# One decoder layer on one core: the router's statistics tile by tile and its rows six slots later, routing in five groups instead of four, the count five slots behind the ranks

## The chip, the core and the metric

The kernel runs on one core of a Trainium2 chip. Five engines run side by side, each its own queue in order, and wait for each other by semaphores: TensorE (PE, matmuls and transposes into eight PSUM banks), VectorE (DVE), ScalarE (ACT), GpSimd (POOL), and SyncE (SP), which issues DMAs. The metric is the device time of one execution in microseconds; less is better. Before the change it is 1469.41 us, the median of three runs (1467.95 to 1471.85).

## The reference

Eight sequences of 256 tokens with 512 features pass three residual blocks. Cut to what matters:

```python
x = x + ssm(layernorm(x))                          # state-space mixer, 64 heads
x = x + xattn(layernorm(x), ctx_512, ctx_512)      # 32 query heads, 8 key heads of 16
x = x + moe(layernorm(x))                          # 8 experts, two per token
# moe: router_input = x * rsqrt(mean(x*x) + 1e-6) * rsqrt(512) * router_scale
#      logits  = router_input @ router_logits       (512 x 8)
#      choices = top 2 of the logits;  weights = softmax probabilities / their sum over the two
#      tokens sorted by expert;  out = (gelu(x Wg) * (x Wu)) Wd * scale, added back by weight
```

All of it is float32 in the kernel's matmuls but for the attention scores, whose queries and keys are split in float16 parts.

## The kernel before, in words

The 2048 tokens are 16 tiles of 128 rows, two tiles per sequence b. All of x stays on the chip. Three stages follow each other: the mixer (to about 700 us), attention and routing (700 to 1014 us), the experts (39 tiles of gathered tokens, to the end).

The order of work is written out by hand. `attention_slots` builds a table from slot numbers to pieces of work, `put(s, piece, ...)` adds pieces to slot s, and every engine walks the same list and does its own part of each piece. So a piece's slot decides where it stands in the queue of each engine that has a part in it; what it waits for is in its code. Inside a slot the pieces stand in the order in which `put` was called. Slots 0 to 255 are the 256 score items, 32 for each sequence (`n = 32`). I call slots 32k to 32k+31 round k. In round k

- TensorE does one `score` (L1033) for sequence k and one `max` (L1018, two matmuls, for sequence k+1) per slot, and one `product` (L1042, eight matmuls in two groups of four heads' quads) for four slots;
- ScalarE does one `exponent` (L1114) per slot, VectorE one `max_fold` (L1216) per slot, both one slot behind;
- the row maxima of sequence k+1 end at slot 27 of the round: `nmax` and `n_turn` at slot 28, `n_copy` and its DMA `n_out` (L1458) at 29. The first score of round k+1 waits for that DMA;
- queries and keys of sequence k+2 are prepared: `q`, `q_hi`, `q_lo`, `q_turn`, `k_turn` and their copies in slots 2 to 24; in rounds 0, 2 and 4 VectorE also takes the layer norm statistics (`q_bn`) of four tiles.

The router's work on sequence b follows in round b+1, counted from f = 32(b+1): GpSimd adds the attention's result to x (`attend`, f+8); VectorE takes the statistics of both tiles (`r_stats`, f+12: two `bn_stats` L1252, two `bn_aggr` L1255, three small ones); GpSimd does three Newton steps for the reciprocal root (`r_newton`, f+12, 14 small instructions); ScalarE writes the normed rows of tile t (`r_xn`, L1133, f+16+2t), SyncE stores them (`r_store`); TensorE turns them (`r_turn`, L540, f+17+2t), ScalarE copies (`r_copy`, L1145), TensorE multiplies by the router's weights (`r_logit`, L1059, eight matmuls shown, f+19+2t), VectorE keeps the eight logits (`r_keep`, L1275). SyncE also writes x of both tiles to the output (`out_in`, f+20). For sequence 6 the rows start seven slots later (`late = 7`).

Routing is done in groups of tiles, `ROUTED = [(last sequence, first tile, end), ...]`. A group is a chain of small VectorE instructions: `c_scale` (and `c_newton` on GpSimd), `c_rank` (eight instructions, L1307 to L1314, whose size grows with the tiles), `c_count` (two matmuls on TensorE that wait for `c_rank`, L1068), `c_logit`, `c_exp` (ScalarE), `c_slots` (L1334 to L1341, one step per tile and five more), `c_weight` (five, L1322 to L1326). `place` (GpSimd, L1363) makes one 128x128 matrix per tile and choice. The last group and the last sequence's router come after slot 265, in a tail that ends with the first gather of tokens for the experts.

Five PSUM banks (`work_ps`) are dealt out in this order by `shared_banks`: a piece that opens a bank takes the one whose last reader stands earliest in the list, and TensorE waits for that reader. So TensorE can run at most a few `max` ahead of VectorE's `max_fold`.

## Time and profile before

| | |
|---|---|
| median of three runs | 1469.41 us (1467.95 to 1471.85) |
| profiled execution, its own time | 1465.78 us |
| its span from first to last instruction | 1464.0 us |
| mean granted TensorE clock | 0.954 of full |
| busy in the span: PE, DVE, ACT, POOL | 92%, 60%, 49%, 40% |
| rounds 0 to 7, start to start, us | 34.3, 34.3, 37.9, 34.1, 44.5, 35.8, 35.2, 27.9 |

How to read it: the span is what the profile measures, 1.8 us less than the execution's own time. The shares of the whole span say little about one stage: in the experts' stage PE is busy nearly all the time, while in the rounds of attention PE and DVE take turns at being the last to be ready. The rounds' lengths are the distances of their first exponents.

### The profile page before, as it was taken

To read this page: it belongs to the slowest core of one execution; us is meant where nothing else is said; L and a number is where in the kernel's file an instruction comes from. 1 tells how busy PE (TensorE), PEld (TensorE's weight loads), DVE (VectorE), ACT (ScalarE), POOL (GpSimd) and SP (SyncE) were. 2 spreads that over 40 slices of the span, in tenths; PEclk is the share of its full clock that TensorE was granted. 3 is DMA by queue.
4 is the path that set the end of the run, shared out by engine and by line. 5 is a ranking of instruction groups with operands and counts; after the bars stand their busy time and mean duration, and the time that the engine had idled before them with its cause. 6 is when DMAs were issued, how large, how long until landed. Compare 5 with 4: busy or idle time off the path is not lost.

```text
span 1464.0 us, 23008 instructions
## 1 busy us (share of the span) xinstructions
PE 1339.8 (92%) x7713; PEld 734.7 (50%) x7713; DVE 877.2 (60%) x1822; ACT 723.4 (49%) x1390; POOL 584.7 (40%) x871
## 2 busy tenths in 40 slices
PE   5799999999999999998788877888999999999997
PEld 4566666666666665654333333323444444444443
DVE  5798898979797979757888888755111111111111
ACT  2666667667666776663676766672111111111110
POOL 1454465555455465774223246143122222222221
PEclk9899999999999999998798988887999999999999
DMA  9000000000000000000210100002343344244322
GB/s 337 9 8 5 7 6 1 12 1 12 1 9 4 8 6 8 17 1 1 97 34 33 35 33 31 30 31 74 115 132 107 79 133 135 51 130 130 58 44 30
DMA packets 40291, 73.00 MB, mean 50 GB/s; under 512 B 18544, under 2 KB 22896, under 8 KB 39152
## 3 DMA queue, kind: packets, MB, share of 16 engines
q1 hardware_dynamic: 30240, 48.10, 9.4%
q0 software_dynamic: 8736, 20.61, 7.3%
q10 hardware_dynamic: 1200, 2.82, 0.5%
q8 instruction: 65, 1.06, 0.3%
q14 instruction: 50, 0.41, 0.1%
HBM read 148.91 MB, written 19.99 MB: 115 GB/s over the span
## 4 chain that ended last, share of the span: by engine, by line
PE 67%; DVE 18%; issue 5%; POOL 3%; ACT 3%; DMA 2%; SPq 1%; POOLq 0%; DVEq 0%; ACTq 0%
PE work_ps L535 13%; PE gate_ps L1524 9%; PE up_ps L1524 9%; PE down_ps L1508 9%; PE work_ps L607 7%; DVE conv L816 6%; PE work_ps L540 3%; PE work_ps L629 3%; DVE maxes L1216 3%; PE work_ps L1042 2%; PE mturn_ps L540 2%; PE decay_ps L1033 2%; PE decay_ps L617 2%; DVE mix L732 2%; DMA qT<-nmaxT 1%
## 5 line engine op out<-in xcount | busy, mean ns | idle before, releaser
L535 PE MATMUL work_ps<-xnT,w_in 128*128 128x256 f32 (+1 forms) x1216 | 301.0, 393 | 2.3 <-DVE xdt L856 1.5
L732 POOL TENSOR_TENSOR mix<-decay,cbm 128x512 f32<-128x512 f32 x128 | 182.1, 1424 | 218.9 <-ACT decay L727 191.0
L535 PEld LDWEIGHTS work_ps<-xnT,w_in 128*128 128x128 f32 (+1 forms) x1216 | 220.2, 189 | 64.9 <-issue 33.7
L723 ACT ACTIVATE decay<-decay_ps 128x512 f32<-128x512 f32 x256 | 154.1, 602 | 111.1 <-PE decay_ps L617 110.5
L1612 POOL DMA_INDIRECT out_dram<-y_out,ids x39 | 61.9, 1587 | 334.3 <-DVE row_w L1576 230.2
L1216 DVE TENSOR_REDUCE maxes<-work_ps 128x2 f32<-128x512 f32 x256 | 166.7, 683 | 42.8 <-PE work_ps L1018 41.8
L816 DVE SCALAR_TENSOR_TENSOR conv<-raw,conv_w,conv 128x256 f32<-128x256 f32 x240 | 179.2, 753 | 7.1 <-ACT conv L683 1.3
L1114 ACT ACTIVATE prob<-decay_ps 128x512 f32<-128x512 f32 x256 | 142.9, 608 | 78.9 <-PE decay_ps L1033 77.5
L1591 DVE TENSOR_TENSOR act<-gelu,up_ps 128x512 f32<-128x512 f32 x39 | 26.8, 688 | 252.1 <-PE up_ps L1524 252.1
L727 ACT ACTIVATE decay<-decay 128x512 f32<-128x512 f32 x256 | 164.0, 641 | 4.7 <-PE work_ps L535 3.0
L1524 PE MATMUL gate_ps<-w_e,xgT 128*128 x312 | 140.5, 593 | 1.4 <-ACT xgT L1541 1.0
L1508 PE MATMUL down_ps<-w_e,actT 128*128 x312 | 140.4, 593 | 0.8 <-ACT actT L1554 0.8
L1524 PE MATMUL up_ps<-w_e,xgT 128*128 x312 | 140.3, 592 | 0.0
L607 PE MATMUL work_ps<-w_out,yz 128*128 128x512 f32 x256 | 131.3, 637 | 4.5 <-DVE yz L874 3.7
L732 DVE TENSOR_TENSOR mix<-decay,cbm 128x512 f32<-128x512 f32 x128 | 102.5, 801 | 34.8 <-PE work_ps L629 19.2
L1033 PE MATMUL decay_ps<-qT,kT 49*128 49x512 f16 x256 | 94.0, 430 | 13.2 <-DMA qT<-nmaxT 8.2
L1583 DVE TENSOR_SCALAR y_out<-down_ps,row_w 128x512 f32<-128x512 f32 x39 | 29.3, 751 | 122.3 <-PE down_ps L1508 122.3
L1018 PE MATMUL work_ps<-kT,qT 48*128 48x256 f16 x512 | 94.2, 302 | 5.1 <-DVE maxes L1216 1.3
L1524 PEld LDWEIGHTS up_ps<-w_e,xgT 128*128 128x128 f32 x312 | 59.3, 190 | 74.6 <-issue 74.6
L629 PE MATMUL work_ps<-mix,xdt 128*32 128x128 f32 x2048 | 83.7, 282 | 8.4 <-DVE mix L732 7.6
L1541 ACT ACTIVATE xgT<-mturn_ps 128x512 f32<-128x512 f32 x39 | 23.3, 597 | 136.6 <-PE mturn_ps L540 136.6
L1042 PE MATMUL work_ps<-prob,v_aug 128*32 128x512 f32 x512 | 81.8, 716 | 9.6 <-DVE maxes L1216 8.9
(270 smaller groups left out, 1913.5 us busy)
## 6 DMA issues: line engine op xcount, KB each, us to landing
w_e<-c_experts_dram SPq DMA_DIRECT2D x39, 3072.0 KB
normed_tokens<-r_xn SPq DMA_DIRECT2D x17, 256.0 KB, 2.2
out_dram<-x_sb SPq DMA_DIRECT2D x17, 256.0 KB, 2.5
x_sb<-x_dram SPq DMA_DIRECT2D x1, 3072.0 KB, 16.6
w_in<-c_w_inT_dram ACTq DMA_DIRECT2D x1, 2560.0 KB, 12.3
w_in<-c_w_inT_dram SPq DMA_DIRECT2D x1, 2048.0 KB, 8.8
w_out<-c_w_outT_dram SPq DMA_DIRECT2D x1, 2048.0 KB, 21.6
RT<-cum_scratch SPq DMA_DIRECT2D x32, 48.0 KB
```

Of the source, the lines that this page charges most:

```text
L535: m = e.matmul(ps[0:width, at:at + L], w_in[:, k, col:col + width], xnT[b % 2][:, k, :], start=(k == 0), stop=(k == KD - 1))
L607: m = e.matmul(work(stage, tile)[:, :], yz[tile % 2][:, ct, :], w_out[:, ct, :], start=(ct == 0), stop=(ct == NCZ - 1))
L629: m = e.matmul(work("y", b, c, hf)[32 * quad:32 * quad + 32, ct * P:(ct + 1) * P], xdt[hf][:, 2 * HG * ct + h, :], mix[(s - 1 + h // HG) % ...
L723: e.activation(decay[s % 5][:, :], decay_ps[s % 3][:, :], ACT.Relu, scale=-1.0).then_inc(piece_done[stage], 1)
L727: e.activation(decay[s % 5][:, :], decay[s % 5][:, :], ACT.Exp, scale=-1.0).then_inc(piece_done[stage], 1)
L732: return e.tensor_tensor(four(mix[s % 5]), four(decay[s % 5]), cb, ALU.mult)
L816: m = e.scalar_tensor_tensor(o, raw[n % 2][:, i, k:k + L], conv_w[:, c, k:k + 1], o, ALU.mult, ALU.add)
L1033: e.matmul(score_ps[s % 3][:, :], kT[b % 3][base:base + PARTS + 1, k, t * P:(t + 1) * P], qT[b % 3][base:base + PARTS + 1, 2 * k:2 * k + 2 ...
L1114: e.activation(prob[s % 12][:, :], score_ps[s % 3][:, :], ACT.Exp, scale=DH ** -0.5).then_inc(piece_done[stage], 1)
L1216: e.reduce_max(maxes[b % 2][:, t, first:first + 2], work("max", b, p)[:, :].rearrange("p (h t) -> p h t", h=2), AX.X).then_inc(piece_done[ ...
L1508: m = e.matmul(down_ps[i % 2][:, :], actT[i % 2][:, k, :], w_e[:, bass.ds(place[i], 1), k, 2 * EH:].rearrange("p o n -> p (o n)"), start=( ...
L1524: m = e.matmul(ps[:, :], xgT[i % 2][:, k, :], w_e[:, bass.ds(place[i], 1), k, off:off + EH].rearrange("p o n -> p (o n)"), start=(k == 0), ...
```

## The change

Only the table of slots changes, and how the statistics are cut.

- `r_stats` is cut: the two `bn_stats` become pieces `r_bn` of their own at f+13 and f+15, one tile each, and `r_stats` (the `bn_aggr` and what follows) and `r_newton` move from f+12 to f+16.
- The router's rows and all that follows them (`r_xn`, `r_store`, `r_turn`, `r_copy`, `r_logit`, `r_keep`, `out_in`) move six slots later for sequences 0 to 5. Sequence 6 keeps its seven.
- `ROUTED` gets five groups. The first one of eight tiles at slot 148 (round 4, slot 20) is cut in two of four tiles, at slots 96 and 160 (rounds 3 and 5, slot 0). The group of tiles 8 to 11 stays at slot 224 (round 7, slot 0), that of 12 and 13 at slot 251, the last one in the tail.
- In the first three groups `c_count` and what follows stand five slots later than before relative to `c_rank`, and `c_weight` is 16 slots behind the group's start instead of 9. `place` follows each group at 17 slots from its start, eight in ten slots, instead of two every four slots.

```diff
-ROUTED = [(3, 0, 8), (5, 8, 12), (6, 12, 14), (7, 14, 16)]
+ROUTED = [(1, 0, 4), (3, 4, 8), (5, 8, 12), (6, 12, 14), (7, 14, 16)]
...
-        late = 7 if b == NB - 2 else 0
-        put(f + 12, ("r_stats", b), ("r_newton", b))
+        late = 7 if b == NB - 2 else 6
+        for t in range(TPB):
+            put(f + 13 + 2 * t, ("r_bn", b, t))
+        put(f + 16, ("r_stats", b), ("r_newton", b))
         for t in range(TPB):
             put(f + 16 + late + 2 * t, ("r_xn", b, t), ("r_store", b, t))
...
-    for g, at in enumerate((4 * n + 20, 7 * n, 7 * n + 27)):
+    for g, (last, first, end) in enumerate(ROUTED[:-1]):
+        at = n * (last + 2) if last < NB - 2 else 7 * n + 27
+        apart = 5 if last < NB - 2 else 0
         put(at, ("c_scale", g), ("c_newton", g))
-        put(at + 3, ("c_rank", g), ("c_count", g))
-        put(at + 5, ("c_logit", g), ("c_exp", g))
-        put(at + 6, ("c_slots", g))
-        if g < 2:
-            put(at + 9, ("c_weight", g), ("c_weight_out", g))
-    for t in range(12):
-        for c in range(2):
-            put(n * 5 + 4 * t if t < 8 else n * 7 + 8 + 4 * (t - 8) + 2 * c, ("place", c, t))
+        put(at + 3, ("c_rank", g))
+        put(at + 3 + apart, ("c_count", g))
+        put(at + 5 + apart, ("c_logit", g), ("c_exp", g))
+        put(at + 6 + apart, ("c_slots", g))
+        if apart:
+            put(at + 11 + apart, ("c_weight", g), ("c_weight_out", g))
+            for t in range(first, end):
+                for c in range(2):
+                    put(at + 12 + apart + 3 * (t - first) + c, ("place", c, t))
...
+            elif stage == "r_bn":
+                b, t = key
+                e.wait_ge(*done("attend", b))
+                own.settle(e.bn_stats(r_bn[:, t, :], x_sb[:, b * TPB + t, :]))
             elif stage == "r_stats":
                 b, = key
-                e.wait_ge(*done("attend", b))
-                for t in range(TPB):
-                    m = e.bn_stats(r_bn[:, t, :], x_sb[:, b * TPB + t, :])
-                own.settle(m)
                 for t in range(TPB):
                     m = e.bn_aggr(r_mv[:, b * TPB + t, :], r_bn[:, t, :])
```

The changed file is five lines longer above the engines' code, so a line L1114 of the kernel before is L1119 after.

Where it moves instructions, first on VectorE in round 1 (sequence 0): the statistics `r_bn`, `r_mv`, `r_rows` among the folds of the maxima (`maxes`) and the copies of keys, queries and outputs. Before:

```order
L1216 TENSOR_REDUCE maxes<-work_ps 128x2
L1252 BN_STATS r_bn<-x_sb 128x6 x2
L1255 BN_AGGR r_mv<-r_bn 128x2 x2
L530 TENSOR_SCALAR r_rows<-r_mv 128x2
L513 TENSOR_SCALAR r_rows<-r_rows 128x2
L514 TENSOR_SCALAR r_rows<-r_rows 128x2
L1216 TENSOR_REDUCE maxes<-work_ps 128x2
```

After:

```order
L1256 BN_STATS r_bn<-x_sb 128x6
L1211 COPY kT<-work_ps 128x8x128
L1221 TENSOR_REDUCE maxes<-work_ps 128x2 x2
L1256 BN_STATS r_bn<-x_sb 128x6
L1239 RECIPROCAL recip<-work_ps 128x16
L1247 TENSOR_TENSOR o_tok<-work_ps,recip 128x2x2x16 x4
L1221 TENSOR_REDUCE maxes<-work_ps 128x2
L1260 BN_AGGR r_mv<-r_bn 128x2 x2
L535 TENSOR_SCALAR r_rows<-r_mv 128x2
L518 TENSOR_SCALAR r_rows<-r_rows 128x2
L519 TENSOR_SCALAR r_rows<-r_rows 128x2
```

One block of seven instructions between two folds has become three blocks, with three folds, a key copy and an output piece between them.

Then on TensorE, round 1 again: the turn of the router's rows (`work_ps<-ident,r_xn`) and the router's matmul (`w_router`). Before, with queries (`ident,xnT`) and keys of the next sequences around them:

```order
L540 MATMUL work_ps<-ident,r_xn 128x128 x4
L540 MATMUL work_ps<-ident,xnT 128x128 x8
L1033 MATMUL decay_ps<-qT,kT 128x512
L1018 MATMUL work_ps<-kT,qT 128x256 x2
L1042 MATMUL work_ps<-prob,v_aug 32x512 x4
L1033 MATMUL decay_ps<-qT,kT 128x512
L1018 MATMUL work_ps<-kT,qT 128x256 x2
L1059 MATMUL work_ps<-w_router,r_xnT 128x8 x4
L540 MATMUL work_ps<-ident,r_xn 128x128 x4
L1033 MATMUL decay_ps<-qT,kT 128x512
```

After, with the turn of the maxima (`nmax`) behind them:

```order
L1064 MATMUL work_ps<-w_router,r_xnT 128x8 x4
L545 MATMUL work_ps<-ident,r_xn 128x128 x4
L1038 MATMUL decay_ps<-qT,kT 128x512
L1023 MATMUL work_ps<-kT,qT 128x256 x2
L1047 MATMUL work_ps<-prob,v_aug 32x512 x4
L1038 MATMUL decay_ps<-qT,kT 128x512
L1023 MATMUL work_ps<-kT,qT 128x256 x2
L1064 MATMUL work_ps<-w_router,r_xnT 128x8 x4
L1038 MATMUL decay_ps<-qT,kT 128x512
L1023 MATMUL work_ps<-kT,qT 128x256 x2
L1029 MATMUL work_ps<-ident,nmax 32x128 x2
```

The router's two turns and two products have left the stretch in which queries are turned, and stand in the round's last eight slots, right ahead of the turn of the maxima.

Last, ScalarE in round 1, the rows `r_xn` and their copies `r_xnT` among the exponents (`prob`). Before:

```order
L1133 ACTIVATE r_xn<-x_sb,r_rows 128x512
L1114 ACTIVATE prob<-decay_ps 128x512 x2
L1145 ACTIVATE r_xnT<-work_ps 128x512
L1133 ACTIVATE r_xn<-x_sb,r_rows 128x512
L1114 ACTIVATE prob<-decay_ps 128x512
L1108 ACTIVATE qT<-work_ps 128x8x128
```

After:

```order
L1107 ACTIVATE xbc<-xn 128x32x16
L1119 ACTIVATE prob<-decay_ps 128x512 x4
L1113 ACTIVATE qT<-work_ps 128x8x128
L1119 ACTIVATE prob<-decay_ps 128x512
L1126 ACTIVATE pv<-work_ps 128x512
L1119 ACTIVATE prob<-decay_ps 128x512 x2
L1138 ACTIVATE r_xn<-x_sb,r_rows 128x512
```

Six more exponents, a query copy and an output copy now stand ahead of the first row.

## Rows read from the trace of the kernel before

**Rows 1.** Windows: length, PE, PEld, DVE, ACT, POOL busy, clock, DMA; rounds, or stretches.

```profile
742.84:763.75 20.91, 18.45 (x167) 9.69 (x171) 17.63 (x42) 15.95 (x30) 8.46 (x20) 0.92 0.17 57
763.75:771.04 7.29, 4.78 (x43) 1.76 (x37) 6.06 (x15) 4.73 (x10) 0.00 (x0) 1.00 0.02 5
771.04:808.89 37.85, 31.93 (x253) 14.24 (x251) 30.84 (x77) 26.51 (x50) 13.13 (x38) 0.86 0.10 33
778.54:802.27 23.73, 20.72 (x170) 10.27 (x171) 18.06 (x45) 16.05 (x29) 10.22 (x28) 0.84 0.15 51
808.89:842.96 34.07, 27.29 (x253) 12.98 (x251) 28.92 (x68) 26.40 (x50) 10.42 (x24) 1.00 0.11 37
842.96:887.48 44.52, 33.88 (x255) 14.54 (x251) 39.22 (x112) 26.98 (x52) 17.23 (x52) 0.82 0.09 28
893.82:917.55 23.73, 19.67 (x167) 10.61 (x171) 18.50 (x42) 16.28 (x30) 18.34 (x34) 0.86 0.12 46
929.10:952.03 22.93, 19.04 (x112) 9.13 (x112) 13.96 (x36) 12.04 (x24) 5.06 (x16) 0.73 0.12 46
```

**Rows 2.** Chain that ended last, in round 1: start us, us, what.

```profile
746.27 1.21 DVE r_bn L1252 x2
...
752.02 0.23 POOL r_rows L1371
752.28 0.82 ACT r_xn L1133
...
767.23 3.34 DMA qT<-nmaxT
```

**Rows 3.** Waits, 702 to 990 us: who waited for whom, us in total, times, longest.

```profile
PE decay_ps L1033 <- DMA qT<-nmaxT: 8.2, 6, 1.9
...
PE work_ps L1024 <- DVE nmax L1222: 6.4, 6, 3.0
ACT r_xn L1133 <- POOL r_rows L1371: 5.9, 6, 2.7
...
PE work_ps L540 <- ACT r_xn L1133: 5.7, 6, 2.7
...
PE work_ps L1068 <- DVE chosen L1312: 3.7, 2, 3.5
...
ACT weight L1150 <- DVE weight L1298: 2.1, 2, 1.0
```

**Rows 4.** PE in order of time, round 1: router's matmuls and a turn, full clock.

```profile
755.89 1.06 PE L1059 MATMUL work_ps<-w_router,r_xnT 128*128 128x8 f32 x8
756.80 0.64 PE L540 MATMUL work_ps<-ident,r_xn 128*128 128x128 f32 x4
```

**Rows 5.** PE in order of time, round 6: the same two at half clock.

```profile
942.00 1.87 PE L1059 MATMUL work_ps<-w_router,r_xnT 128*128 128x8 f32 x8
943.73 1.09 PE L540 MATMUL work_ps<-ident,r_xn 128*128 128x128 f32 x4
```

**Rows 6.** DVE in order of time, round 7: a four-tile group, first and last of its steps.

```profile
957.21 0.15 DVE L1281 TENSOR_TENSOR mean_sq<-r_rows 128x4 f32<-128x4 f32 x1
...
958.08 0.42 DVE L1307 TENSOR_TENSOR larger<-logit 128x256 f32<-128x256 f32 x1
...
960.41 0.17 DVE L1314 TENSOR_SCALAR chosen<-rank 128x32 bf16<-128x32 f32 x1
...
962.14 0.17 DVE L1295 TENSOR_SCALAR mean_sq<-mean_sq 128x4 f32<-128x4 f32 x1 [1.56 <-POOL mean_sq L520]
...
964.63 0.17 DVE L1341 SCALAR_TENSOR_TENSOR place_of<-rounded,slot_of 128x8 f32<-128x8 f32 x1
...
965.53 0.18 DVE L1322 TENSOR_TENSOR weight<-weight,chosen 128x32 f32<-128x32 f32 x1
...
966.18 0.83 DVE L1325 TENSOR_TENSOR weight<-weight,mean_sq 128x32 f32<-128x32 f32 x1
967.04 1.19 DVE L1326 TENSOR_TENSOR weight<-weight,e_scale 128x32 f32<-128x32 f32 x1
```

More of the change, by code:

```diff
@@ L170, in mixer_slots @@
     return slots
-DMA_ONLY = {"freed", "mixed", "cum_out", "cum_in", "ctx_in", "n_out", "router_in", "first_expert", "r_store", "out_in", "c_weight_out", "keep_warm"}
+DMA_ONLY = {"freed", "mixed", "cum_out", "cum_in", "ctx_in", "n_out", "router_in", "first_expert", "r_store", "out_in", "c_weight_out", "keep_warm", "r_bn"}
 def bank_use(stage, *key):
@@ L284, in attention_slots @@
         put(f, ("last_stats", t), ("last_center", t))
-    put(f, ("last_newton",), ("c_weight", 2), ("c_weight_out", 2), *[("place", c, t) for t in (12, 13) for c in range(2)])
+    put(f, ("last_newton",), ("c_weight", 3), ("c_weight_out", 3), *[("place", c, t) for t in (12, 13) for c in range(2)])
     for stage in ("r_turn", "r_copy", "r_logit"):
@@ L289, in attention_slots @@
         put(f, ("r_xn", NB - 1, t), ("r_store", NB - 1, t), ("out_in", NB - 1, t), ("r_keep", NB - 1, t))
-    put(f, ("c_rank", 3), ("keep_warm", 1, 5), ("c_count", 3), ("keep_warm", 2, 11), ("c_logit", 3), ("c_exp", 3), ("c_slots", 3), *[("place", c, t) for t in (14, 15) for c in range(2)])
-    put(f, ("c_base",), ("c_spread", 0), ("c_weight", 3), ("c_weight_out", 3), ("c_spread", 1))
+    put(f, ("c_rank", 4), ("keep_warm", 1, 5), ("c_count", 4), ("keep_warm", 2, 11), ("c_logit", 4), ("c_exp", 4), ("c_slots", 4), *[("place", c, t) for t in (14, 15) for c in range(2)])
+    put(f, ("c_base",), ("c_spread", 0), ("c_weight", 4), ("c_weight_out", 4), ("c_spread", 1))
     return slots
```

## The prediction

> **What bounds the kernel now.** I read four things in this order: the windows of the rounds, the waits, the chain of one round, and single instructions in order of time. All that the change moves lies in rounds 1 to 7, so the mixer, the tail behind slot 265 and the experts keep their time, unless their first gather comes at another moment.
>
> In the middle of round 1 (20.91 us) TensorE is busy 18.45 and VectorE 17.63 [rows 1]: neither is the bound alone. They hand the time to each other. Up to the half of it VectorE is behind, since the folds, key copies, output copies and the statistics stand close; then TensorE is, with turns of queries, router rows and router products. The chain says so in round 1: `r_bn` of both tiles on VectorE 1.21, GpSimd's Newton steps to 752.25, the row `r_xn` 0.82 at 752.28, TensorE after it [rows 2]. The waits for this hand-over are ScalarE's for `r_rows`, 5.9 us in six waits, longest 2.7, and TensorE's for `r_xn`, 5.7 in six, longest 2.7 [rows 3]: one delay, told twice.
>
> In the closing (763.75 to 771.04, 7.29 us) TensorE is busy only 4.78 and VectorE 6.06 [rows 1]. There the folds of the maxima, the copy `nmax`, its turn, and the DMA `n_out` (3.34 us in round 1 [rows 2]) stand behind each other; the first score of the next round waits 8.2 us in six for that DMA, 1.4 each, and the turn of the maxima 6.4 in six for `nmax` [rows 3].
>
> Round 4 is the outlier: 44.52 us against 37.85 for round 2, which has the same other work; VectorE is busy 39.22 against 30.84 [rows 1]. That is the group of eight tiles: 8.4 us of VectorE work cost 6.67 us, 3.5 of it as one wait of TensorE's `c_count` for `chosen` [rows 3].
>
> The clock counts too: mean 0.84 in the middle of round 2, 0.82 in round 4, 0.86 in round 5's middle, 0.73 in round 6's [rows 1]. The router's product took 1.06 us at the full clock (2.4 GHz) and 1.87 at the half (1.2 GHz), a turn 0.64 and 1.09 [rows 4, 5].
>
> **The statistics and the rows, middle.** `r_bn` is the same work in two pieces, one more start: below 0.1 us, I take 0. With the rows six slots later, `r_xn` (slot 22) has some six exponents more between itself and the Newton steps, so the 5.7 us of waits go. The router's two turns and two products (2 x (0.5 + 1.0) = 3.0 us of TensorE at the full clock, taking a turn at 0.5 rather than the 0.64 that overlaps its neighbour) leave the middle, which then holds 15.4 us of TensorE work and is bound by VectorE: its 17.63 plus 1.0 of idle that I leave it. Bounds of that idle: 0, and the 3.3 that it has today. I take 1.0 because VectorE is short of work only where TensorE is behind, and TensorE has 3 us less.
> - Round 1: 17.63 + 1.0 = 18.6, against 20.91: -2.3. Round 3 has the same pieces and nearly the same length: -2.3.
> - Round 2: 18.06 + 1.0, plus 0.7 for statistics of x that wait for GpSimd, = 19.8, against 23.73: -3.9. Round 4 alike, its group apart: -3.9.
> - Round 5: 18.50 + 1.0 = 19.5 against 23.73: -4.2.
> - Round 6: 22.93, less the four pieces at the half clock (2 x (1.87 + 1.09) = 5.9), less 0.5 for the rest of its wait for `r_xn`: 16.5, -6.4. VectorE's 13.96 [rows 1] is no bound.
>
> Sum: -23.0 us.
>
> **The same pieces, closing.** Six closings (rounds 1 to 6) take 3.0 us of TensorE work more. Of round 1's idle (7.29 - 4.78 = 2.5) the wait for `n_out` can't be filled, since the router's products stand ahead of it; the wait for `nmax` (6.4 in six, the longest 3.0, in the others near 0.7) can. So +3.0 - 0.7 = +2.3 each, +13.9 in all. Bounds: +0.5, if all 2.5 of idle filled up, and +5.8, if the clock falls (below). The rows' stores (slots 22 to 26) now stand three to five slots ahead of `n_out` on the same queue, and two rows of 0.82 us on ScalarE stand among the exponents there: 0 to 1 us each, I take 0.3, +1.8 for six.
>
> **The groups.** Round 4 loses its group: -6.7. Rounds 3 and 5 get one of four tiles each. Its price is from round 7's, which has four tiles today [rows 6]: `c_scale` 957.21 to 958.17, 0.96; `c_rank` 958.08 to 960.58, 2.5; `c_logit` and `c_slots` 962.14 to 964.80, 2.7; `c_weight`, five instructions of 0.2 where nothing disturbs them, 1.0: 7.2 us of VectorE in all. What idle is there for it? In round 3 VectorE is busy 28.92 of 34.07; of the 5.15 idle I count 3.3 in the middle and 1.2 in the closing by round 1's rows, so 0.65 is left in the opening, where the group stands. To that comes about 0.8 at the round's start, in which VectorE waits for the DMA, and 0.5 of the middle's idle for `c_weight`: 7.2 - 0.65 - 0.8 - 0.5 = 5.2. Twice: +10.4. Round 4's own rate (6.67 for 8.4) would give 5.7 each. Together +3.7: two small groups in the stretches where VectorE is the bound cost more than a large one where it had some room. This step speaks against the change, and is half of why I forecast little.
>
> In round 7 `c_count` now stands five slots behind `c_rank` and `c_logit` behind the Newton steps, for which VectorE waited 1.56 us [rows 6]. ScalarE's wait for `weight` (2.1 in two [rows 3], 1.05 here) and 0.2 of TensorE's for `chosen` go: -1.2.
>
> In `c_weight` L1325 and L1326 took 0.83 and 1.19 us, where L1322, of the same shape, took 0.18; GpSimd was at work on the output's addition and on `place` there [rows 6]. The Trainium skill (SBUF — State Buffer, section "Who interferes with whom") says that a VectorE instruction with two SBUF inputs contends with a GpSimd instruction that reads SBUF; the trace agrees. If `c_weight` in rounds 3 and 5 met such work it would be 2.7 us instead of 1.0, and the sum 3.4 us higher. In the new order `place` stands a slot behind `c_weight` and can't start ahead of its place in the queue, and the addition (slot 8) is over; I leave it out.
>
> **The sum.** -23.0 + 13.9 + 1.8 + 3.7 - 1.2 = -4.8 us. The profiled execution took 1465.78 itself (its span 1464.0), so it would take 1461.0. The median of the runs shown is 1469.41, 3.6 above it; the difference carries over: 1464.6 us.
>
> **The rivals.** One in which nothing of this applies, that the rows aren't freed: `r_newton` ends where today's ended plus four slots, the rows start six later, so two slots are gained, about 2.3 us in a middle, against waits of 0.95 in the mean and 2.7 at most. Enough; only round 6 could keep 0.4 us. No rival with a chance of its own.
>
> *The clock falls in the closings (slower).* TensorE would be at 0.5 in the closings where VectorE has starved it ahead: rounds 3 and 5 (groups) and round 6, which is at 0.89 and below already. Then a closing's 7.8 us of TensorE work takes 1.87/1.06 = 1.76 times as long, +5.9; 1.8 to 2 of it lies under waits for `nmax` and `n_out` that shrink, so +3.9 each, +11.7 for three: 1476. For it: the half clock stands behind stretches in which TensorE waited, as in the middle of round 6 after 2.7 for `r_xn`. Against: the closing of round 1 had the clock 1.00 with only 4.78 of 7.29 busy [rows 1], and will be fuller. It decides from two closings on. The Trainium skill (TensorE: Matmul & The Clock Gate, section "What's actually happening") holds that the throttled clock is the default and activity releases it; round 1's closing, at 1.00 while a third idle, is no example of that rule either way, and the rule would make the fuller closing safe. Chance 0.20.
>
> *What leaves the middle comes back (same).* VectorE keeps 1.8 us of idle in each middle rather than 1.0, since the folds' banks tie it to TensorE slot by slot: +0.8 x 6 = +4.8, 1469.4. For it: today's idle is 3.3 with both engines near 18. Against: TensorE has 3 us less there. Chance 0.21.
>
> *The half clock goes (larger gain).* In rounds 4 and 6 it follows long waits, 3.5 for `chosen` and 2.7 for `r_xn`, which the change removes. If those stretches run at 2.4 GHz throughout, the rest of the two rounds' matmuls gains about 3 us each: 1458.5. Against: round 2 falls to 0.84 with no such wait. Chance 0.14.
>
> **How the numbers follow.** The forecast has 0.45, with its own range 1460 to 1468. A difference under 0.3% (4.4 us) can't be told from none here; the forecast lies just past that, so I give 0.29 of it to faster, 0.16 to the same. Faster: 0.29 + 0.14 + 0.01 of the second rival = 0.44. Same: 0.16 + 0.20 + 0.01 of the first = 0.37. Slower: 0.19. The range of 8 in 10: 1455, beyond the larger gain with its own error, to 1475, which leaves out half of the slower case.
>
> **What would show it.** In the profile after: no wait of `r_xn` for `r_rows`; no wait near 3.5 of `c_count`; rounds 1 to 7 of 34.6, 36.6, 39.6, 36.5, 39.4, 31.4 and 26.7 us; in the closings TensorE busy 7.8 at a granted clock near 1.00, and 9 to 10 us long. Closings of 12 or a clock of 0.5 there mean the first rival; middles of 19.5 us in rounds 1 and 3 the second; clocks of 1.00 in rounds 4 and 6 the third. The forecast is wrong in its largest term if the closings grow by less than 1 us, since 13.9 rests on TensorE having no room there; and in the groups if rounds 3 and 5 don't grow by 4 us and more.

## The result, and the profile after

| | before | changed |
|---|---|---|
| median, runs of the first comparison | 1470.63 us (4 runs, 1467.95 to 1476.6) | 1486.19 us (4 runs, 1484.51 to 1490.97) |
| ratio, 95% interval | | 1.0124 (1.0095 to 1.0154) |
| repeated on another occasion | 1466.26 us (29 runs) | 1476.14 us (12 runs, 1466.75 to 1490.89), ratio 1.0065 (1.0029 to 1.0101) |
| span of the profiled execution | 1464.0 us | 1484.5 us |
| its mean granted TensorE clock | 0.954 | 0.936 |

I forecast 1464.6 us, faster; it is slower by 0.65 to 1.2%. Of the 20.5 us between the two spans, 5.7 had arisen before round 0 began (round 0 starts at 702.41 and at 708.15 us), where no instruction was changed. Rounds 0 to 7 account for 14.6 more (284.0 against 298.6 us), the tail and the experts for 0.2. So about a quarter of the distance between these two profiles arose where the change moves nothing: ahead of round 0 the same instructions ran at a mean granted clock of 0.96 instead of 0.97. The medians in the table are of all runs; the ratios leave out the runs over 1.5% above the fastest of their kernel (two of the changed kernel's twelve).

First windows of the kernel before that were not shown: rounds 1, 5, 6 and 7, and the closings of rounds 2 and 5 (columns as in [rows 1]: length, then PE, PEld, DVE, ACT, POOL busy, the granted clock).

```profile
736.75:771.04 34.29, 28.28 (x253) 13.32 (x251) 29.11 (x68) 26.39 (x50) 10.45 (x24) 0.95 0.11 36
887.48:923.30 35.82, 29.89 (x253) 14.33 (x252) 29.47 (x68) 26.83 (x51) 21.27 (x38) 0.89 0.09 31
923.30:958.50 35.20, 29.38 (x191) 12.54 (x188) 23.90 (x66) 21.49 (x40) 6.03 (x19) 0.81 0.08 31
958.50:986.41 27.91, 23.73 (x138) 8.70 (x138) 15.88 (x74) 20.90 (x42) 16.47 (x48) 0.90 0.11 40
...
802.27:808.89 6.62, 4.79 (x43) 1.76 (x37) 5.47 (x14) 4.74 (x10) 0.00 (x0) 1.00 0.02 5
...
917.55:923.30 5.75, 4.79 (x43) 1.70 (x37) 5.31 (x14) 4.73 (x10) 0.00 (x0) 1.00 0.02 6
```

The same view of the changed kernel, rounds 1 to 7:

```profile
740.78:778.40 37.62, 33.45 (x253) 14.23 (x251) 29.14 (x68) 26.97 (x51) 10.46 (x24) 0.82 0.09 33
778.40:820.88 42.48, 38.46 (x253) 16.08 (x249) 30.84 (x77) 26.93 (x50) 13.18 (x38) 0.72 0.08 29
820.88:863.53 42.65, 34.63 (x252) 14.46 (x254) 35.73 (x100) 27.37 (x53) 19.64 (x44) 0.84 0.09 30
863.53:901.57 38.04, 32.57 (x253) 14.30 (x251) 31.68 (x83) 27.04 (x50) 13.19 (x38) 0.87 0.09 33
901.57:947.08 45.51, 39.07 (x255) 16.64 (x251) 35.61 (x94) 27.50 (x51) 19.46 (x44) 0.74 0.07 25
947.08:976.20 29.12, 24.96 (x190) 10.18 (x188) 24.43 (x67) 21.49 (x42) 6.59 (x21) 0.96 0.10 38
976.20:1006.76 30.56, 26.54 (x138) 8.90 (x138) 15.62 (x73) 21.00 (x42) 15.86 (x46) 0.78 0.11 36
```

Compare rounds 1 and 2 with the rows before. VectorE has nearly the same work (29.11 and 29.14, 30.84 and 30.84), and TensorE shows the same 253 matmuls, but is busy 33.45 instead of 28.28 and 38.46 instead of 31.93: the work is the same and the mean clock is lower, 0.95 to 0.82 and 0.86 to 0.72. How much of a round's length is the clock and how much the new order, these rows alone don't tell. With two levels, 0.5 and 1, a mean of 0.72 over 42.48 us is 23.8 us at the half clock. Summed over rounds 1 to 7 that makes about 57 us before and 101 after.

Where I had put the gain and the loss, the changed kernel's middles of rounds 1, 2 and 6, and the closings of rounds 1, 2, 5 and 6 behind them:

```profile
748.71:768.65 19.94, 17.57 (x151) 8.08 (x148) 17.63 (x41) 15.45 (x28) 7.39 (x19) 0.91 0.04 14
768.65:778.40 9.75, 8.35 (x58) 3.44 (x60) 5.81 (x15) 5.62 (x12) 0.00 (x0) 0.82 0.23 84
786.26:809.39 23.13, 20.36 (x151) 9.10 (x148) 18.02 (x41) 15.79 (x29) 9.99 (x27) 0.78 0.03 12
809.39:820.88 11.49, 11.32 (x58) 4.75 (x58) 5.14 (x14) 5.42 (x11) 0.00 (x0) 0.55 0.20 71
935.61:947.08 11.47, 11.30 (x58) 4.77 (x58) 5.14 (x14) 5.43 (x11) 0.00 (x0) 0.55 0.20 71
953.01:967.96 14.95, 12.07 (x96) 4.86 (x97) 14.38 (x36) 11.21 (x22) 5.08 (x16) 1.00 0.05 20
967.96:976.20 8.24, 7.99 (x50) 3.36 (x49) 4.49 (x19) 5.55 (x12) 0.81 (x3) 0.87 0.26 97
```

Before, the middle of round 1 was 20.91 and its closing 7.29 [rows 1]. The closings of rounds 2 and 5 are TensorE busy for all but 0.17 us of 11.5, at 0.55 of the clock. Round 6's middle, where half clock went (0.73 before, 1.00 now), is 8.0 us shorter.

The changed kernel has a second profile (after_again below, its own time 1486.49 us). In it the closings of all of rounds 1 to 5 are like those two. Here are rounds 1, 3 and 5; rounds 2 and 4 took 11.1 us at 0.56:

```profile
761.72:773.25 11.53, 11.29 (x58) 4.73 (x58) 5.14 (x14) 5.43 (x11) 0.00 (x0) 0.56 0.23 82
847.03:858.54 11.51, 11.29 (x58) 4.74 (x58) 5.14 (x14) 5.43 (x11) 0.00 (x0) 0.56 0.21 76
935.68:947.18 11.50, 11.33 (x58) 4.76 (x58) 5.15 (x14) 5.43 (x12) 0.00 (x0) 0.55 0.20 71
```

The closings of rounds 1 to 6 add up to 45.0 us before and to 59.0 and 65.1 in the two profiles of the changed kernel.

The waits that the change was to remove are gone or small (columns: us in total, times, longest; 708 to 1007 us), against 5.9, 5.7 and 6.4 in [rows 3]:

```profile
ACT r_xn L1138 <- POOL r_rows L1376: 1.4, 1, 1.4
PE work_ps L545 <- ACT r_xn L1138: 0.8, 1, 0.8
PE work_ps L1029 <- DVE nmax L1227: 0.7, 1, 0.7
```

And the half clock in the chain that ended last, round 1 (start us, us, what): the same product of eight matmuls at either level, and the DMA of the maxima, 2.48 us here behind the rows' stores against 3.34 in [rows 2].

```profile
759.33 1.86 PE work_ps L1047 x8
...
764.06 0.99 PE work_ps L1047 x8
...
770.16 1.86 PE work_ps L1047 x8
...
775.44 2.48 DMA qT<-nmaxT
```

### The profile page after: what moved, and what is told of

Read it like the earlier page. It is cut to its first block, busy times and chain, and to the rows that moved or that the text cites. A ratio compares the mean times of both kernels' runs of the same rounds, so it can differ in the third digit from the quotient of the medians.

```text
span 1484.5 us, 23067 instructions
## 1 busy us (share of the span) xinstructions
PE 1368.6 (92%) x7715; PEld 741.2 (50%) x7715; DVE 880.8 (59%) x1849; ACT 725.4 (49%) x1391; POOL 588.0 (40%) x883
## 4 chain that ended last, share of the span: by engine, by line
PE 69%; DVE 18%; issue 5%; ACT 3%; DMA 2%; POOL 1%; SPq 1%; POOLq 0%; DVEq 0%; ACTq 0%
PE work_ps L540 13%; PE gate_ps L1529 9%; PE up_ps L1529 9%; PE down_ps L1513 9%; PE work_ps L612 7%; DVE conv L821 6%; PE work_ps L545 3%; PE work_ps L1047 3%; PE work_ps L634 3%; DVE maxes L1221 3%; PE mturn_ps L545 2%; PE decay_ps L1038 2%; PE decay_ps L622 2%; PE work_ps L1023 2%; DVE mix L737 1%
## 5 line engine op out<-in xcount | busy, mean ns | idle before, releaser
L1119 ACT ACTIVATE prob<-decay_ps 128x512 f32<-128x512 f32 x256 | 144.4, 604 | 100.4 <-PE decay_ps L1038 98.8
L1023 PE MATMUL work_ps<-kT,qT 48*128 48x256 f16 x512 | 102.2, 316 | 17.2 <-DVE maxes L1221 8.4
L1038 PE MATMUL decay_ps<-qT,kT 49*128 49x512 f16 x256 | 99.7, 452 | 10.2 <-DMA qT<-nmaxT 6.5
L1047 PE MATMUL work_ps<-prob,v_aug 128*32 128x512 f32 x512 | 89.5, 779 | 0.7 <-ACT prob L1119 0.7
```

The costliest lines, as they stand in the source:

```text
L1023: m = e.matmul(work(*piece)[:, hh * L:(hh + 1) * L], qT[b % 3][base:base + PARTS, 2 * k + hh, t * P:(t + 1) * P], kT[b % 3][base:base + PA ...
L1047: m = e.matmul(work("pv", b, s % N_ITEMS // 8)[32 * q:32 * q + 32, :], v_aug[b % 2][:, t, 4 * kh + q, :], prob[(s - 3 + q) % 12][:, :], st ...
L1119: e.activation(prob[s % 12][:, :], score_ps[s % 3][:, :], ACT.Exp, scale=DH ** -0.5).then_inc(piece_done[stage], 1)
```

## The experiments

Times are medians; "clock" is the median over the runs of the mean granted clock. The kernel before lay at 1466.3 to 1469.9 us and 0.950 to 0.953 in the comparisons. Each row is compared with runs of the kernel before on the same occasion; between occasions the ratios compare better than the medians. after_light leaves out three quarters of the router's product, so its logits are other ones by design. Expected and measured follow one by one below.

| kernel | us | runs | ratio to before (95%) | clock |
|---|---|---|---|---|
| shift_only | 1469.4 | 10 | 1.0018 (0.9993 to 1.0043) | 0.948 |
| groups_only | 1470.0 | 10 | 1.0016 (0.9983 to 1.0050) | 0.952 |
| rows_only | 1463.7 | 10 | 0.9962 (0.9933 to 0.9991) | 0.953 |
| rows_again (the same) | 1466.0 | 12 | 1.0000 (0.9962 to 1.0037) | 0.952 |
| after_again | 1476.1 | 12 | 1.0065 (1.0029 to 1.0101) | 0.946 |
| after_warm | 1485.0 | 4 | 1.0131 (1.0086 to 1.0177) | 0.944 |
| after_fill | 1470.0 | 12 | 1.0034 (1.0006 to 1.0062) | 0.959 |
| after_fill_closing | 1477.0 | 9 | 1.0074 (1.0048 to 1.0099) | 0.956 |
| after_light | 1473.3 | 12 | 1.0058 (1.0030 to 1.0085) | 0.944 |
| after_groups_late | 1482.0 | 6 | 1.0117 (1.0064 to 1.0170) | 0.942 |
| after_burst | 1468.2 | 12 | 1.0011 (0.9980 to 1.0041) | 0.951 |
| after_cut_early | 1472.2 | 12 | 1.0040 (1.0016 to 1.0064) | 0.950 |
| after_burst_late | 1481.9 | 6 | 1.0100 (1.0059 to 1.0141) | 0.942 |
| before_fill | 1466.2 | 12 | 0.9988 (0.9964 to 1.0012) | 0.963 |
| rows_fill | 1461.8 | 12 | 0.9976 (0.9946 to 1.0005) | 0.962 |
| rows_later | 1458.2 | 12 | 0.9925 (0.9889 to 0.9960) | 0.953 |
| rows_later_fill | 1468.3 | 12 | 0.9970 (0.9939 to 1.0001) | 0.956 |

**The parts alone.** Three kernels made from the one before; where the rows move, the group of eight tiles has to move with them.

rows_only is this diff, shift_only this and the cut of the statistics, groups_only the changed groups alone.

```diff
-        late = 7 if b == NB - 2 else 0
+        late = 7 if b == NB - 2 else 6
...
-    for g, at in enumerate((4 * n + 20, 7 * n, 7 * n + 27)):
+    for g, at in enumerate((4 * n + 26, 7 * n, 7 * n + 27)):
...
-            put(n * 5 + 4 * t if t < 8 else n * 7 + 8 + 4 * (t - 8) + 2 * c, ("place", c, t))
+            put(n * 5 + 6 + 3 * t if t < 8 else n * 7 + 8 + 4 * (t - 8) + 2 * c, ("place", c, t))
```

> The kernel before with the statistics cut and the router's rows six slots later, and its four old groups, of which the one of eight tiles has to move with the rows (slot 154 instead of 148). Theory S (the shift costs, since the closings grow and more of the time is spent at the half clock): rounds 1 and 2 as in the changed kernel, near 37.6 and 42.5 us, round 3 near 37.4, round 6 near 29; 8 to 11 us slower in all, about 1479 to 1482. Theory G (the two small groups are what costs, the lengths of rounds 1 and 2 after are a chance of that profile's clock): rounds 1 and 2 near 34.5 and 37, no slower than before, 1464 to 1472.

> The kernel before with the five new groups and their new distances alone; statistics and rows stay where they were. Theory S: rounds 1, 2 and 6 as before (34.3, 37.9, 35.2); rounds 3 and 5 up by 5 each, round 4 down by 7, round 7 up by up to 2.7: 3 to 6 us slower, 1473 to 1477. Theory G: rounds 3 and 5 up by 8 each, the whole 10 to 15 us slower, 1480 to 1486.

> As the kernel with the shift alone, but the statistics stay one burst of seven instructions at slot 12 of the round. It tells the cut from the shift. Theory S expects within 2 us of the kernel with the shift alone, since the price is in the closings. Rival: the cut and the later statistics (slots 13 to 16, where query copies stand) are what hold the folds back; then rounds 1 and 2 are 1.5 us or more shorter here than with the cut.

The shift's profiled execution had rounds 1 and 2 of 37.7 and 42.5 us as theory S says, but it was its second slowest; its median is only 0.2% up. The groups alone are up 0.2% as well; in their profile rounds 3 to 5 sum to 119.1 us against 114.4, +4.7 where I had forecast +3.7, but at a mean clock of 0.86 against 0.90. Both intervals reach 1. Neither part is the 1.2% of the first comparison; their sum, 0.34%, lies inside the interval of the second (0.29 to 1.01%), so a loss that only the two together bring isn't shown. Unexpected is the third: with the statistics in one burst at slot 12, the shift is 5.8 us faster than with the statistics cut and later (ratios 0.9962 and 1.0018, intervals apart). rows_again, a repetition, took back its apparent gain on the kernel before:

> The rows six slots later, statistics in one burst at slot 12, four groups, once more and unchanged: it had 1463.7 us against 1467.6, ratio 0.996 (0.993 to 0.999). If that is a gain and not luck, a ratio of 0.994 to 0.998 again; if luck, 0.999 to 1.003.

With both sets the rows' shift alone lies between 0.996 and 1.000; a gain isn't shown. The profile of rows_again shows what the shift is worth, since its round 3 is at the full clock (whole, middle, closing):

```profile
808.98:842.04 33.06, 27.57 (x253) 12.95 (x251) 28.76 (x68) 26.70 (x51) 10.43 (x24) 1.00 0.11 38
815.07:833.61 18.54, 15.66 (x148) 7.76 (x148) 17.54 (x41) 15.46 (x29) 8.44 (x20) 1.00 0.04 16
833.61:842.04 8.43, 6.87 (x58) 3.33 (x60) 5.81 (x15) 5.53 (x12) 0.00 (x0) 1.00 0.27 98
```

Against 34.07 us before, also at the full clock [rows 1], that is 1.0 us a round. A closing at the half clock takes 11.5 us instead of 8.4 and eats up three such rounds. Where the rows stay in the middle, in the profiles of before, groups_only and before_fill, the closings of rounds 1, 2, 3 and 5 are at 1.00 in 12 of 12. In the nine profiles with the rows six slots later, all of the router's product and no thrown-away matmuls, the same four closings are at 0.60 or less in 18 of 36: 5 of 16 where the statistics stand at slots 12 and 13, 13 of 20 where they come later. That is one execution each, or two of the changed kernel, so it shows the direction and not the size.

**The changed kernel again, and with TensorE kept busy.** The matmuls of ones write into the bank that the next score overwrites. In after_warm `WARM = 6` of them stand ahead of the wait for the DMA; `FILL` is (9, 21, 1) in after_fill, before_fill and rows_fill, (20, 32, 1) in after_fill_closing.

```diff
+                if s % N_ITEMS == 0 and s:
+                    e.wait_ge(*done("exponent", s - 3))
+                    for _ in range(WARM):
+                        e.matmul(score_ps[s % 3][:, :], m_ones[:, :], m_ones[:, :].rearrange("p (o j) -> p o j", o=1).to_broadcast([P, 4, P]), start=True, stop=True)
...
+                if 1 <= b < NB - 1 and FILL[0] <= s % N_ITEMS < FILL[1]:
+                    for _ in range(FILL[2]):
+                        e.matmul(score_ps[s % 3][:, :], m_ones[:, :], m_ones[:, :].rearrange("p (o j) -> p o j", o=1).to_broadcast([P, 4, P]), start=True, stop=True)
```

> The changed kernel once more, nothing edited. Its four runs lay at 1484 to 1491 us with a mean granted clock of 0.936 to 0.941; the shift alone and the groups alone each lay near 1469 to 1470 in ten runs, with single ones up to 1481 and 1485 at the same low clocks, and the shift's profiled one has the same rounds 1 and 2 (37.7 and 42.5) as the changed kernel's. Theory I (the two parts together bring a loss that neither brings alone): again 1480 or more, ratio 1.009 to 1.015. Theory P (the clock's low stretches fall by the luck of each execution, and the first four of the changed kernel fell badly): median 1470 to 1476, spread over 15 us and more, ratio 1.001 to 1.006.

Theory P, but for a hair: 1476.14 us, a ratio of 1.0065 and a spread of 24 us. The interval (1.0029 to 1.0101) leaves room for a part of I. The slower the run, the lower its clock: 1490.89 us at 0.935, 1466.75 at 0.953.

> The changed kernel with six matmuls of ones (128x512, bf16, about 1.3 us at the full clock) ahead of the first score of rounds 1 to 7, in the time in which TensorE waits for the DMA of the maxima (1 to 1.9 us after the products of the round are done). They are thrown away. If the half clock is what the change costs and waiting brings it on, the share of half clock in rounds 1 to 7 falls and the kernel gains 4 us or more on the changed one, up to 1482 or less. If the clock only tells of waits whose time is lost anyway, or the openings are not where it is decided, 1486 to 1490: nothing gained, at most 1 us for each round lost where the six stand in the way.

Between the two bands: 1485.0 us in four runs shows no gain, though its profile has rounds 1 and 4 at 33.2 and 35.3 us without any half clock.

> The changed kernel with one thrown-away matmul of ones (128x512, bf16, 0.22 us) ahead of each of the scores of slots 9 to 20 of rounds 1 to 6, 2.6 us a round: about the TensorE work that the change took out of that stretch, which VectorE bounds. If the emptier middle is what brings the half clock on, rounds 1 and 2 get shorter than 37.6 and 42.5 by 2 us and more and the kernel gains 5 us on the changed one. If the clock doesn't depend on it, the work is in the way: 0 to 2.6 us a round slower, up to +12.

As the first reading says: 6.2 us faster than the changed kernel, with some 16 us of TensorE work more in it (the means of the runs differ by 8.3 us, give or take 4.9). Round 1 of its profile, its middle and its closing, at the full clock throughout:

```profile
733.79:767.91 34.12, 31.00 (x265) 13.63 (x263) 29.02 (x68) 27.21 (x51) 10.48 (x24) 1.00 0.10 36
739.89:759.53 19.64, 19.00 (x163) 8.47 (x162) 17.80 (x41) 15.96 (x29) 8.49 (x20) 1.00 0.04 14
759.53:767.91 8.38, 6.87 (x58) 3.33 (x60) 5.80 (x15) 5.53 (x12) 0.00 (x0) 1.00 0.27 98
```

At the full clock the twelve aren't free: the middle is 19.64 us here and 18.54 without them (rows_again above), 1.1 for 2.6 of work. What they gain in this profile is clock, and in the middles: the closings of rounds 2 and 4 still took 11.4 and 11.0 us.

> The control for the thrown-away matmuls: the same twelve a round, but ahead of the scores of slots 20 to 31, where TensorE has the most work, instead of 9 to 20. If what helped was TensorE being fuller where VectorE holds it back, they cost their 2.6 us a round here or most of it: 8 to 16 us above the changed kernel, 1484 to 1492. If any more TensorE work in the round does (a rival), 1468 to 1473 as with slots 9 to 20.

Between the two: the clock rises to 0.956 here too, but the time stays at the changed kernel's. More work raised the clock in both places; it paid only where VectorE leaves TensorE idle.

> The kernel before with the twelve matmuls at slots 9 to 20. There the router's turns and products still stand in slots 17 to 21. If only the change's emptied middle needs them, no gain or a loss of up to 1 us a round: 1466 to 1473. If the kernel before also pays for its half clock (72 us of it in rounds 0 to 7 in its profile), up to 4 us faster, 1462 to 1465.

The clock rises most of all (0.953 to 0.963) and the time doesn't move (0.9988, 0.9964 to 1.0012). That fits a half clock that is paid for mainly where TensorE is last; in the kernel before most of it lies elsewhere, with the closings of rounds 1, 2, 3 and 5 at 1.00. It doesn't prove it: the twelve may also have cost what the clock gave back.

**The closings and the groups.**

First the diff of after_light, then of after_groups_late.

```diff
+                ks = KD if b == NB - 1 else 1
-                for k in range(KD):
+                for k in range(ks):
...
-        at = n * (last + 2) if last < NB - 2 else 7 * n + 27
+        at = n * (last + 2) + (11 if last < 4 else 0) if last < NB - 2 else 7 * n + 27
```

> The changed kernel with the router's product of sequences 0 to 6 over one fourth of the features (2 matmuls shown instead of 8 for each tile, 0.75 us less): the logits are other ones, so another routing. 1.5 us of TensorE work leave each of the six closings. If TensorE has no room there, as I forecast (2.3 of 3.0 us paid), it gains 1.1 to 1.5 us a round, 7 to 9 us; more, up to 15, where the closings run at the half clock. If the closings wait for VectorE and the DMA anyway, under 2 us.

2.9 us less than the changed kernel, which is between the two, and the intervals overlap: inconclusive on its own. The room is better read from a closing at the full clock (below).

> The changed kernel with its first two groups eleven slots later in rounds 3 and 5 (slots 11 to 27 instead of 0 to 16). Openings of 10.1 and 8.2 us should fall to 6.1 and 6.3, as in rounds without a group. If the price of a group is VectorE's work where VectorE has no idle (my reading), c_rank at slot 14 still lies in such a stretch, but c_logit, c_slots and c_weight fall where TensorE is the bound: rounds 3 and 5 shorter by 2 to 4 us each, 4 to 8 us in all. If the groups cost their work wherever they stand: same within 2 us.

The second reading, or worse: the openings fell to 6.1 in both rounds, but the middles grew to 27.2 and 28.7 us, and the whole is no faster. In round 3 the middle's 4.3 us more undo the opening's 4.0 less, so the group's work was only moved. Round 5's middle ran at a clock of 0.64 and tells less.

**The cut, or the place of the statistics.** Four arrangements of the same seven instructions, all else as changed: one burst at slot 12, pieces at 12 and 13, pieces at 13, 15 and 16 (the changed kernel), one burst at 16. The diff is after_burst's; after_burst_late has `f + 16` there, after_cut_early `f + 12 + t` and `f + 13` in the pieces' two lines.

```diff
-        for t in range(TPB):
-            put(f + 13 + 2 * t, ("r_bn", b, t))
-        put(f + 16, ("r_stats", b), ("r_newton", b))
+        put(f + 12, ("r_stats", b), ("r_newton", b))
```

> The changed kernel with the statistics back in one burst at slot 12 (the seven instructions together, the Newton steps behind them), rows and groups as changed. Without the groups that was 1463.7 against 1469.4 us with the cut, medians of ten. If the cut costs by itself (three blocks of statistics where VectorE has no room, the Newton steps late), 4 to 7 us faster than the changed kernel, ratio to before near 1.002. If that difference was the luck of the clock, 1474 to 1478 again.

> The changed kernel with the statistics cut as changed, but at slots 12 and 13 (what follows them at 13) instead of 13, 15 and 16. Theory L (the later place costs): as with the burst at slot 12, 1466 to 1471 us, TensorE idle in round 1 mostly in slots 12 to 15 and slots 16 to 19 near 4.3 us long instead of 6.9. Theory C (the cut itself costs): 1474 and more.

> The changed kernel with the statistics uncut, all at slot 16. Theory L: slow as the changed kernel, 1474 to 1486, with TensorE idle 1.5 us or more in slots 16 to 19 of round 1 and half clock in rounds 1 and 2 well over 10 us in all. Theory C: 1466 to 1471.

1468.2, 1472.2, 1476.1 (1486.2 in the first set), 1481.9: the order is that of the place, and the uncut burst at slot 16 is the worst. The comparison that changes the place alone is the first against the last: ratios of 1.0011 and 1.0100, whose intervals are apart. So theory L holds for the larger part. The cut at slots 12 and 13 fell between the two theories, and its slots 16 to 19 took 5.69 us at a clock of 0.70, where L had said 4.3. Its 4 us over the burst at slot 12 are inside overlapping intervals: a cost of the cut by itself isn't shown. Now slots 12 to 15 and 16 to 19 of round 1, after_burst:

```profile
743.72:748.56 4.84, 3.25 (x30) 1.46 (x30) 4.67 (x15) 3.42 (x8) 3.00 (x13) 1.00 0.00 0
748.56:752.80 4.24, 3.90 (x39) 1.74 (x38) 4.19 (x9) 3.44 (x6) 2.40 (x6) 1.00 0.02 4
```

after_burst_late:

```profile
742.75:746.23 3.48, 3.18 (x32) 1.57 (x32) 3.44 (x10) 3.32 (x8) 1.54 (x3) 1.00 0.00 0
746.23:751.82 5.59, 3.83 (x39) 1.68 (x36) 5.41 (x14) 3.56 (x6) 3.46 (x14) 1.00 0.01 3
```

The changed kernel:

```profile
752.32:755.79 3.47, 3.18 (x30) 1.46 (x30) 3.44 (x6) 3.31 (x8) 1.52 (x3) 1.00 0.00 0
755.79:762.73 6.94, 5.43 (x36) 1.95 (x35) 5.51 (x18) 3.56 (x6) 3.88 (x16) 0.75 0.01 2
```

VectorE is busy nearly throughout in all of them, and TensorE idles where the statistics stand: 1.6 us in slots 12 to 15 with the early burst, 1.8 and 1.5 in slots 16 to 19 with the late ones. In these eight slots, at the full clock, the place costs nothing: slots 12 to 19 take 9.08 us with the early burst and 9.07 with the late one. In the changed kernel, which had the half clock in the second piece, they take 10.41. That the 13 us between the two bursts are the clock's is argued from this and from their mean clocks (0.951 and 0.942), not shown apart.

> The rows six slots later, statistics in one burst, four groups (the one of eight tiles at slot 154), and the twelve matmuls at slots 9 to 20. Without them 1463.7 at a clock of 0.953, ten runs from 1454 to 1476. If the fill takes away the low clock here too, 1456 to 1462, below both kernels, and a spread under 15 us. If the burst at slot 12 leaves no room for them, 1463 to 1470.

1461.8 us, inside the upper edge of the expected band and 2 to 4 us below rows_only and rows_again, less than their intervals can tell; against the kernel before the interval still reaches 1.0005.

**Statistics and rows later still.** From the kernel before; the places of the eight tiles start at slot 5 n + 10, three slots apart.

```diff
-        late = 7 if b == NB - 2 else 0
-        put(f + 12, ("r_stats", b), ("r_newton", b))
+        late = 7 if b == NB - 2 else 10
+        put(f + 12 if b == NB - 2 else f + 21, ("r_stats", b), ("r_newton", b))
...
-    for g, at in enumerate((4 * n + 20, 7 * n, 7 * n + 27)):
+    for g, at in enumerate((4 * n + 30, 7 * n, 7 * n + 27)):
```

> The kernel before with the statistics of sequences 0 to 5 in one burst at slot 21 and the rows ten slots later, four groups (the one of eight tiles at slot 158). If it is the place ahead of the stretch bounded by TensorE that hurts, slot 21 doesn't: the copies of the traces show VectorE idle 0.7 in slots 20 to 23 and 3.6 in 24 to 27, so middles near 18 us and 1455 to 1466 in all. If later is worse in itself, since the router's work then meets the end of the round and the next opening, 1470 to 1485.

The best kernel of the study: 0.75% below the one before, and below the changed one, at the same clock as before (0.953 to 0.950). The windows of its round 3 (whole, then closing) and of round 1 (middle, closing):

```profile
802.19:832.97 30.78, 27.79 (x253) 13.07 (x251) 28.07 (x68) 26.27 (x50) 10.45 (x24) 1.00 0.10 33
737.80:753.88 16.08, 14.21 (x136) 6.55 (x137) 15.82 (x38) 13.48 (x26) 7.88 (x17) 0.99 0.00 1
753.88:768.51 14.63, 14.63 (x72) 7.55 (x71) 7.19 (x19) 7.42 (x15) 0.61 (x4) 0.50 0.24 83
824.36:832.97 8.61, 8.54 (x71) 4.72 (x71) 6.83 (x19) 7.08 (x14) 0.60 (x4) 1.00 0.18 67
```

Round 3 is 30.8 us at the full clock, against 33.06 with the rows six slots later and 34.07 before. The statistics haven't left the middle: they stand in slots 20 to 23 of it. There they no longer cost time of their own. Slots 12 to 19 and 20 to 23 of round 1, with the burst's first piece, and slots 20 to 23 of after_burst:

```profile
741.41:744.88 3.47, 3.17 (x32) 1.57 (x32) 3.44 (x10) 3.32 (x7) 1.52 (x3) 1.00 0.00 0
744.88:748.42 3.54, 3.52 (x39) 1.63 (x36) 3.49 (x7) 3.43 (x6) 1.15 (x2) 1.00 0.02 5
748.42:753.88 5.46, 4.15 (x34) 1.77 (x33) 5.29 (x17) 3.12 (x7) 2.12 (x11) 0.97 0.00 0
...
748.68 1.27 DVE L1252 BATCH_NORM_STATS2 r_bn<-x_sb 128x6 f32<-128x512 f32 x2
...
752.80:758.64 5.84, 5.14 (x46) 2.96 (x44) 5.07 (x13) 5.00 (x10) 0.00 (x0) 1.00 0.12 45
```

Slots 12 to 19 fall from 9.08 to 7.01 us without the statistics, and slots 20 to 23, which took them in, are no longer than in after_burst, since the first row's turn and product (1.5 us of TensorE) left them. What VectorE is late by ends in the closing: it is busy 6.83 there instead of 5.81, and the closing takes 8.61 us against 8.43. So the gain belongs to the two moves together; no run parts the place of the statistics from that of the rows. A closing with the same pieces took 14.63 us at 0.50 (round 1) and 8.61 at 1.00 (round 3): 6.0 us is what one closing pays for the half clock when TensorE is last.

> The same with the twelve thrown-away matmuls at slots 9 to 20. By the earlier pairs (changed kernel 1476 to 1470, rows alone 1464 and 1466 to 1462, kernel before 1467 to 1466) 1 to 6 us faster than without them, clock 0.96; if the middle has lost its starved stretch, they cost up to 5 us instead.

10 us slower: the same matmuls are in the way. Round 3's middle took 18.59 us with them, at the full clock, against 16.08 in rows_later: here nearly all of their 2.6 us is paid.

I read the results so: moving the rows out of the middle is worth its 1.0 us a round at the full clock, and puts work into closings that then often run at the half clock, 3.1 us each. The later statistics go with more of that. Rows and statistics later still are worth 3.3 us a round at the full clock (30.78 against 34.07).

## Why the prediction was wrong, point by point

Rounds 1 to 7 as a whole (before, after_burst, and the two profiles of the changed kernel); my sum for them was 244.8 us:

```profile
736.75:986.41 249.66, 204.38 (x1581) 90.65 (x1577) 197.33 (x530) 175.50 (x332) 95.00 (x242) 0.89 0.10 33
734.01:981.38 247.37, 207.13 (x1583) 88.84 (x1579) 201.47 (x549) 178.54 (x333) 98.88 (x254) 0.90 0.10 34
740.78:1006.76 265.98, 229.67 (x1583) 94.79 (x1579) 203.06 (x557) 178.30 (x333) 98.37 (x254) 0.81 0.09 31
733.90:1007.01 273.11, 238.60 (x1583) 98.37 (x1579) 203.57 (x557) 178.00 (x332) 99.11 (x254) 0.79 0.09 30
```

after_burst has my rows and my groups, with the statistics at slot 12. In its fastest run, at the clock of before, the sum was 2.6 us off. In the changed kernel it was 21 and 28 us off, at 0.81 and 0.79. The rounds that I missed by most are 2 (36.6 forecast, 42.5 measured) and 5 (39.4 and 45.5).

**The rows and the middles: right at the full clock.** I forecast 18.6 us for round 1. after_burst, at the full clock, measured 18.54, with TensorE busy 15.65 where I had 15.4:

```profile
740.10:758.64 18.54, 15.65 (x148) 7.75 (x148) 17.54 (x41) 15.47 (x29) 8.48 (x20) 1.00 0.04 15
```

The changed kernel had 19.94 there at 0.91, and 23.13 against my 19.8 in round 2 at 0.78. Round 6 gave -8.0 for my -6.4. The waits for `r_rows` and `r_xn` went as I said.

**The closings: mis-sized, too high at the full clock, too low at the half.** I took +2.6 each with the stores. At the full clock they are 8.38 (after_fill, round 1) against 7.29, and 8.43 (rows_again, round 3) against 7.08: +1.1 and +1.35. TensorE is busy 6.87 there, 2.1 more than before and not 3.0, since the first tile's turn and its product both run ahead of the closing's first exponent (759.53 in after_fill), which I overlooked:

```profile
756.73 0.66 PE L546 MATMUL work_ps<-ident,r_xn 128*128 128x128 f32 x4
...
758.12 1.03 PE L1068 MATMUL work_ps<-w_router,r_xnT 128*128 128x8 f32 x8
```

The 0.3 us for the stores doesn't show either: the DMA of the maxima took 2.48 us behind them in round 1, less than the 3.34 before. In the changed kernel the closings of rounds 2 and 5 took 11.5: +4.9 over 6.62 and +5.7 over 5.75.

**The groups: right in size.** +3.7 forecast, +4.7 in the profile of the groups alone, with more half clock in it, so the 1 us between them can't be read. `c_weight` stayed undisturbed, 0.19 us for L1330 and L1331 in round 5, as I had assumed.

**The statistics "in two pieces, I take 0": wrong.** At the full clock the cut itself shows as 0.1 us: the middle of round 1 took 18.63 us in after_warm, with the statistics cut as changed, and 18.54 in after_burst. But this step also moved the statistics from slot 12 to slots 13 to 16, and cut and place together were worth 8 us between medians (1468.2 to 1476.1), the place alone, from slot 12 to 16, 13. I counted the instructions and their number, and not where TensorE would idle because of them.

**The clock: the step that failed.** My forecast priced every closing at the full clock and carried the rest of the clock over from before. The first rival had the mechanism, with 0.20; I spoke for safety with "the closing of round 1 had the clock 1.00 with only 4.78 of 7.29 busy, and will be fuller". The runs showed the opposite: the fuller closings ran at 0.55 to 0.56, in rounds 2 and 5 of one profile and 1 to 5 of the other, and took 11.1 to 11.5 us, 3.1 over the 8.4 of the full clock (the rival had said +3.9). TensorE was busy 11.32 of 11.49 us in one of them, so being full didn't protect it. The rival had named rounds 3, 5 and 6, behind the groups; the half clock came without groups too (shift_only: 11.5 in rounds 2, 3 and 5), and in openings (rounds 1 and 7: 7.9 and 8.8 us instead of 6.1).

How much of the loss is it? All 16 runs of the changed kernel have a mean of 1481.3 us at 0.9424, and 132 runs of the one before, from the experiments' comparisons, 1467.7 at 0.9515. Between the runs of one kernel 0.01 of clock goes with 9.1 us (before) and 12.0 us (changed). So the 0.0091 between them go with 8 to 11 of the 13.6 us; 3 to 5 us remain at equal mean clock, where I had forecast a gain of 4.8. The mean clock doesn't tell on which stretch the half clock falls, and in the changed kernel it falls on closings, where TensorE is last. This is a relation between runs, not a proof for each microsecond; what acts on the clock and helps is after_fill. The forecast's distance from the first four runs (1486.2) holds luck as well: the next twelve had a median of 1476.1.

**What stays open.** Why the half clock comes in the closings once the rows stand there, and oftener with the later statistics. It often stands behind stretches in which TensorE idled, but after_burst_late had 1.8 us of idle in slots 16 to 19 of round 1 and kept 1.00 through both of its rows above. The runs of one kernel spread by 20 us and more, so that no single profile shows it. And after_groups_late (1482.0 in six runs) lies above the changed kernel's twelve; with six runs that may be chance, and I can't explain it from its rounds.

## What to carry to other kernels

Where two engines take turns as the bound, cost a moved instruction by the place where the other engine will idle for it: statistics moved four slots later cost 13 us of 1470, and moved nine slots later, together with the rows, they were part of a gain of 12. Where the clock has two levels, forecast each stretch at both (a closing: 8.4 or 11.5 us in the changed kernel, 8.6 or 14.6 in rows_later), and let the range span them: the single profile of before had one draw of them. Take twelve runs, not four, before a difference of under 1% is read.

## What the hardware did that I had not expected

Thrown-away matmuls raised the mean granted clock wherever they stood (0.953 to 0.963 in the kernel before, 0.946 to 0.959 and 0.956 in the changed one), yet the time fell in only one of these three. A closing that had run at the full clock with TensorE busy two thirds of the time (4.80 of 7.08 us, round 3 before) ran at 0.56 once it was full (11.29 of 11.51 us, round 3 of the changed kernel's second profile). One unchanged kernel's runs went from 1459.6 us at a clock of 0.958 to 1479.3 at 0.937.
